# Four transformer layers on one core: biases by TensorE in the joint layers, deviations in eights, the router's places and transfers spread anew, and the first context in eight parts

## Chip, core and metric

One Trainium2 chip, one of its cores. The metric is the time on the device in microseconds (us) of one execution of the whole program. The engines are TensorE (PE in the profile, its weight loads PEld), VectorE (DVE), ScalarE (ACT), GpSimd (POOL) and SyncE (SP), which issues most transfers.

## The reference, cut to what matters

The input x has 64 sequences of 128 tokens with 128 features, the context 64 sequences of 77 tokens. Four layers follow one another, each an attention part and a part of experts:

```
x = x + additive_cross_attention(layernorm(x), context, mask)      # layer 0
x = x + experts16_top4(layernorm(x))                               # layer 0
x = x + cross_attention(layernorm(x), context)                     # layer 1
x = x + experts8_top2(layernorm(x))                                # layer 1
x = x + masked_cross_attention(layernorm(x), context)              # layer 2
x = x + widths_self_attention(layernorm(x))                        # layer 2, its "ffn"
x = x + lowrank_top64_attention(layernorm(x), context)             # layer 3
x = x + experts64_top4_capacity128(layernorm(x))                   # layer 3

# the ends of the two attentions that the change touches
self: outs = xn_o @ o_w[:m, :m].T + o_b[:m]; x = layernorm(x) + outs + x      # 8 heads
low:  out  = (attn @ v) @ Uo @ Vo + bo;       x = x + out                     # 16 heads, top 64 of 77 keys
# the router of the last part
probs = softmax(x @ router_w); top_p, top_i = top_k(probs, 4)
pos = place of each (token, expert) pair among the pairs of its expert; pairs with pos >= 128 go elsewhere
```

A layer norm needs 1/sqrt(var + eps) of every token, that is 64 numbers (one a sequence) in each of 128 partitions.

## The kernel before

The residual stream `X` stays in SBUF, as 64 tiles of 128x128, one a sequence. Each part of a layer is a block of the program in which every engine runs its own written out list of steps, one sequence (or four) a step, and the engines meet through semaphores. A new block begins only when all engines have ended the one before, SyncE with its issues among them.

**Deviations.** VectorE makes mean and variance of all 64 sequences; GpSimd raises them to the power -1/2 (`pow` against a tile of -0.5), since no other engine here does. `norm_gpsimd` (L109) does the first 24 columns (`FIRST`) in the small block that loads the weights, `norm_gpsimd_rest` (L115) the other 40 at the start of the block of steps, ahead of all that GpSimd has to do there. The joint layers need a second power (of the inner norm) and four small operations (`offsets`, L3225 to L3233), on 24 and on 40 columns as well.

**Start.** `load_x` issues the 8 parts of X (L3119), then five constants (L3121). VectorE waits for all constants, makes a bf16 copy of the identity that nothing reads (L3132), and then takes statistics of the 64 sequences (L3136). The block of layer 0's weights (L963) issues nine small loads and then the whole context `l_ctxT`, 2464 KB, in one; the block ends when all have landed, since VectorE waits for them (L980). In layer 0's steps GpSimd adds the text's and the features' halves for half of tanh's input (L1120), which ScalarE waits for (L1068).

**Joint layers** (lines 3155 to 3950). Layer 2's self attention works on sequence a and layer 3's low rank attention on sequence s = a - 9, in the same step, and the router of the last experts runs along in groups of four sequences: c = s // 4 is the group and v = s % 4 the step in it. GpSimd's list in each step is, in this order:

- the router's first part: at v = 0 probabilities and deviations of a group (L2595, L2567 to L2590), at v = 2 `place` (L2614 to L2630), seven operations on 128x256;
- `self_bias(a-2)` (L3762) and `low_bias(s)` (L3766), each 128x128; TensorE waits for both before it adds the results into PSUM with a matmul against the identity (L3415 for the low rank part);
- `self_cut(a+1)` (L3772), for which TensorE waits to project the next self attention;
- `low_distances(s, 0)` (L3778), `self_less_maxima(a)` (L3784), at every fourth step `low_deviations` (L3804 to L3822), `self_spread_k(a+1)` (L3790), `low_distances(s, 1)` (L3778), `low_spread_k(s+1)` (L3797);
- the router's end: at v = 0 `chosen` (L2602, L2609), at v = 2 `fill_rows` (L2636 to L2638), and in each step 4 indirect transfers (L2646), each of which writes 128 rows to the experts' rows in HBM.

The self attention goes round a loop: less maxima(a), then spread k(a+1) on GpSimd, scores(a+1) on TensorE, a copy by ScalarE (L3634), the maxima by VectorE (L3902), less maxima(a+1). VectorE's main work in a step is the selection of the 64 largest of 77 scores for 16 heads in two halves (L3859 to L3886: eight each time), which waits for the distances (L3778).

## Time and profile before

| | |
|---|---|
| time before, median of 3 runs | 3697.84 us (3689.33 to 3698.01) |
| the profiled execution's own time | 3692.36 us |
| its span in the trace | 3690.6 us |
| mean granted clock of TensorE | 0.909 |
| busy: PE, PEld, DVE, ACT, POOL | 2808.8, 1773.2, 2828.7, 2196.2, 2082.5 us |
| start to the first step of layer 0 | 0 to 46.2 us |
| layer 2's cross attention begins | 1867 us |
| joint layers | 2288 to about 3419 us |

The times in all rows are microseconds from the start of the span, unless they say ns. A group of instructions has a line of the kernel, an engine, an operation and its tiles with partitions x elements. A wait in brackets is the time in which the engine was idle before that instruction, and what it was released by. The granted clock is a share of TensorE's full speed.

### The profile page before, as it was taken

How to read it: one execution, taken by the hardware profiler on the slowest of the kernel's cores; microseconds unless marked ns; L12 is line 12 of the kernel's file. 1: busy time of each engine (PE TensorE's matmuls, PEld its weight loads, DVE VectorE, ACT ScalarE, POOL GpSimd, SP SyncE). 2: the span in 40 equal slices, each digit the busy share in tenths (PEclk: the TensorE clock that was granted, in tenths of full speed). 3: DMA queues.
4: the chain of work that ended last, by engine and by line, in shares of the span. 5: the costliest groups of instructions: out<-in, count | busy, mean ns of one | idle time of the engine just before them, and what ended most of it. 6: DMA issues, size and time to landing. Idle time of an engine off the chain costs nothing. (4 is left out here: it accounts for less than half of the span.)

```text
span 3690.6 us, 78369 instructions
## 1 busy us (share of the span) xinstructions
PE 2808.8 (76%) x23589; PEld 1773.2 (48%) x23589; DVE 2828.7 (77%) x11741; ACT 2196.2 (60%) x4429; POOL 2082.5 (56%) x2407
## 2 busy tenths in 40 slices
PE   3777777699979999789669995677777777776267
PEld 1222222344437777544356674455555555554255
DVE  6999999566657788533478885399999999899366
ACT  4999999333326666434246663677677776665130
POOL 5777777200011565747444445545878888777660
PEclk9999999899989999899879997899899998887585
DMA  4332221344420010035410000000111000000037
GB/s 136 119 112 114 100 110 71 83 92 92 92 44 9 27 29 27 31 107 139 123 36 16 15 15 19 3 13 14 40 36 37 21 7 5 5 5 3 1 112 235
DMA packets 179876, 211.46 MB, mean 57 GB/s; under 512 B 73542, under 2 KB 138728, under 8 KB 172039
## 3 DMA queue, kind: packets, MB, share of 16 engines
q1 hardware_dynamic: 146824, 174.31, 16.8%
q0 software_dynamic: 23424, 27.94, 2.3%
q10 hardware_dynamic: 9216, 4.20, 0.4%
q8 instruction: 199, 3.26, 0.4%
q14 instruction: 213, 1.74, 0.2%
HBM read 113.61 MB, written 114.13 MB: 62 GB/s over the span
## 5 line engine op out<-in xcount | busy, mean ns | idle before, releaser
L1068 ACT ACTIVATE l_H<-l_H 128x2048 f32<-128x2048 f32 (+2 forms) x256 | 598.7, 2743 | 2.9 <-POOL l_H L1120 2.7
L1120 POOL TENSOR_TENSOR l_H<-l_feat,l_text 128x4096 f32<-128x4096 f32 x64 | 450.4, 7038 | 131.1 <-PE PS L1024 130.5
L1024 PE MATMUL PS<-l_H,l_wide 128*32 128x512 f32 (+1 forms) x2560 | 330.8, 592 | 164.1 <-ACT l_H L1068 164.1
L1142 DVE TENSOR_TENSOR l_H<-PS,l_text 128x2048 f32<-128x2048 f32 (+1 forms) x192 | 411.7, 2146 | 2.1 <-ACT l_text L1095 2.1
L558 ACT ACTIVATE a_Pr<-PS 77x512 f32<-77x512 f32 x512 | 300.0, 587 | 53.4 <-PE PS L405 53.4
L109 POOL TENSOR_TENSOR RSTD<-norm_tmp,MINUS_HALF 128x24 f32<-128x24 f32 x5 | 20.9, 4190 | 508.6 <-DVE norm_tmp L102 508.6
L2646 POOL DMA_INDIRECT expert_rows<-e3r_row,e3r_rows_at x256 | 254.9, 996 | 89.0 <-issue 74.9
L405 PE MATMUL PS<-IDENT,a_T 128*77 128x128 f32 x2048 | 303.1, 283 | 0.5
L3399 PE MATMUL PS<-IDENT,a_T_l 128*77 128x128 f32 x1024 | 182.2, 308 | 125.3 <-ACT a_Pr_s L3641 101.4
L666 POOL TENSOR_TENSOR a_T<-a_T,a_mx 128x616 f32<-128x616 f32 x128 | 155.6, 1216 | 203.5 <-DVE a_mx L741 203.5
L405 PEld LDWEIGHTS PS<-IDENT,a_T 128*77 128x77 f32 x2048 | 243.0, 153 | 36.7 <-ACT a_yT L544 19.3
L1024 PEld LDWEIGHTS PS<-l_H,l_wide 128*32 128x32 f32 x2560 | 57.4, 109 | 341.1 <-ACT l_H L1068 294.0
L3399 PEld LDWEIGHTS PS<-IDENT,a_T_l 128*77 128x77 f32 x1024 | 129.9, 164 | 179.0 <-ACT a_Pr_s L3641 123.0
L3886 DVE MATCH_REPLACE8 a_T_l<-a_r,a_T_l 128x77 f32<-128x77 f32 x1024 | 213.7, 223 | 0.3 <-issue 0.3
L3867 DVE MATCH_REPLACE8 a_T_l<-a_r,a_T_l 128x77 f32<-128x77 f32 x1024 | 213.7, 223 | 0.3 <-issue 0.3
L2150 POOL DMA_INDIRECT pair_shares<-e_res,e_share_at x156 | 151.6, 972 | 79.7 <-issue 45.1
L3617 ACT ACTIVATE a_Pr_l<-PS 77x512 f32<-77x512 f32 x256 | 151.5, 592 | 74.3 <-PE PS L3399 73.7
L1490 ACT ACTIVATE e_act_g<-PS 128x512 f32<-128x512 f32 x128 | 76.4, 597 | 199.7 <-PE PS L1429 199.5
L3778 POOL TENSOR_TENSOR a_T_l<-a_mx_l,a_T_l 128x616 f32<-128x616 f32 x128 | 155.6, 1216 | 56.4 <-DVE a_mx_l L3896 56.2
L1511 DVE TENSOR_TENSOR e_gu<-e_act_g,PS 128x512 f32<-128x512 f32 x128 | 87.6, 684 | 111.5 <-ACT e_act_g L1490 111.5
L3859 DVE MAX8 a_r<-a_T_l 128x8 f32<-128x77 f32 x1024 | 149.8, 223 | 3.2 <-POOL a_T_l L3778 3.2
L422 PE MATMUL PS<-a_Pr,a_vaug 77*32 77x128 f32 x4096 | 139.4, 276 | 16.9 <-ACT a_OT L597 16.5
(451 smaller groups left out, 8518.6 us busy)
## 6 DMA issues: line engine op xcount, KB each, us to landing
pair_rows<-l_zero SPq DMA_DIRECT2D x35, 1024.0 KB, 5.0
e_wide<-expert_scores SPq DMA_DIRECT2D x32, 1024.0 KB, 9.7
expert_shares<-l_zero SPq DMA_DIRECT2D x16, 1024.0 KB, 5.0
e3c_four<-expert_shares SPq DMA_DIRECT2D x64, 256.0 KB, 3.8
e_xin<-pair_rows SPq DMA_DIRECT2D x39, 264.0 KB, 3.2
e_four<-pair_shares SPq DMA_DIRECT2D x16, 512.0 KB, 4.1
e_w<-in_L_ffn_blocks SPq DMA_DIRECT2D x39, 194.0 KB, 2.5
e3x_xin<-expert_rows SPq DMA_DIRECT2D x32, 200.0 KB
```

The lines of the kernel that those rows point to most:

```text
L405: last = pe.transpose(PS[0:keys, 4 + g % 2, j * S:(j + 1) * S], T[:, u, c:c + keys], m.IDENT[:, :])
L558: act.activation(part, turned, ACT.Exp).then_inc(q[f"P{g}"], 1)
L666: pool.tensor_tensor(t3, t3, bcast(m3, 2, keys), ALU.subtract).then_inc(q[f"T{half}"], 1)
L1024: last = pe.matmul(PS[32 * j:32 * j + 32, 4 + u, 0:cols], wide[:, 32 - r:64 - r], H[:, u, CH * c * S:CH * c * S + cols], start=(r == 0), s ...
L1068: act.activation(cells, cells, ACT.Tanh).then_inc(q[f"tanh{part}"], 1)
L1120: pool.tensor_tensor(H[:, a, lo * S:hi * S].rearrange("p (t f) -> p t f", f=S), bcast(feat[:, a, :], 1, hi - lo), bcast(text[:, a, lo:hi], ...
L1142: dve.tensor_tensor(H[:, u, lo * S:hi * S].rearrange("p (t f) -> p t f", f=S), bcast(PS[:, 1 + u, 0:S], 1, hi - lo), bcast(text[:, u, lo:h ...
L2646: pool.indirect_dma_start(out=m.rows[:, :], out_offset=bass.IndirectOffsetOnAxis(ap=rows_at[:, i % 3, g * K + k:g * K + k + 1], axis=0), i ...
L3399: last = pe.transpose(PS[0:C, 4 + g % 2, j * S:(j + 1) * S], T_l[:, i % 3, c:c + C], m.IDENT[:, :])
L3778: pool.tensor_tensor(t3, bcast(mx_l[:, i % 2, 8 * half:8 * half + 8], 2, C), t3, ALU.subtract) \
L3867: last = dve.match_replace(t3[:, h, :], r1[:, i % 2, 8 * h:8 * h + 8], t3[:, h, :], FAR)
L3886: last = dve.match_replace(t3[:, h, :], r2[:, i % 2, 8 * h:8 * h + 8], t3[:, h, :], FAR)
```

## The change

1. The deviations come in eights: `norm_part(p)` does 8 columns. Part 0 is made in the block of the weights; the others at steps 2, 10, ..., 50 of layers 0, 1 and 2 (at the step's end, ahead of the router's end), all seven in a row at the start of layer 0's experts, and in the joint layers, with the second power and the four small operations, in the GpSimd steps a = 0 to 6, between less maxima(a) and spread k(a+1).
2. The bf16 identity goes, and VectorE's wait for the constants with it. Layer 0's context is issued in eight parts with semaphores of their own, and TensorE waits for a sequence's part.
3. Both biases of the joint layers are added by TensorE, one matmul of the identity and the bias tile each.
4. `place` is split: `slots` stays ahead, `keys` comes after `self_cut`, `far_weights` in the router's end. The 16 transfers of a group go 2, 8, 2, 4 in the steps v = 2, 3, 0, 1, rather than 4 in each.

```diff
-def norm_gpsimd(pool, m): ...
-def norm_gpsimd_rest(pool, m): ...
+def norm_part(pool, m, p):
+    if p == 0:
+        pool.wait_ge(m.s_norm_a, 4 * m.norms + 4)
+    c = slice(EIGHT * p, EIGHT * (p + 1))
+    pool.tensor_tensor(m.RSTD[:, c], m.norm_tmp[:, 0, c], m.MINUS_HALF[:, c], ALU.pow).then_inc(m.s_norm_b, 1)
+def part_due(s):
+    return (s + 6) // EIGHT if s >= 2 and (s + 6) % EIGHT == 0 and s + 6 < B else None
 ...
-            dve.wait_ge(s_const, 16 * len(consts))
-            dve.tensor_copy(m.IDENT_BF[:, :], m.IDENT[:, :])
 ...
-                     (bc[:, 1:2], t[n + "bcb"].partition_broadcast(S)), (ctxT[:, :, :], t["ctxT"])]
+                     (bc[:, 1:2], t[n + "bcb"].partition_broadcast(S))]
+                for p in range(B // EIGHT):
+                    c = slice(EIGHT * p, EIGHT * (p + 1))
+                    sp.dma_start(ctxT[:, c, :], t["ctxT"][:, c, :]).then_inc(q[f"ctx{p}"], 16)
 ...
+                pe.wait_ge(q[f"ctx{i // EIGHT}"], 16)
 ...
+        if have(c - 3 if v >= 2 else c - 4):
+            for k in ((10, 11), range(12, 16), (0, 1), range(2, 10))[v]:
+                scatter(pool, c - 3 if v >= 2 else c - 4, k)
 ...
-                pe.wait_ge(L["bias"], i + 1)
+                pe.matmul(out_ps, m.IDENT[:, :], bo_l[:, :], start=False, stop=False)
                 pe.matmul(out_ps, m.IDENT[:, :], seq(m.X, i), start=False, stop=True).then_inc(L["out"], 1)
 ...
-                pe.wait_ge(Z["y0b"], i + 1)
+                pe.wait_ge(Z["y0"], i + 1)
 ...
+                pe.matmul(out_ps, m.IDENT[:, :], bo_s[:, :], start=False, stop=False)
 ...
             def step(a, s):
                 router.pool_first(pool, s)
-                if real(a - 2):
-                    self_bias(a - 2)
-                if real(s):
-                    low_bias(s)
                 if real(a + 1):
                     self_cut(a + 1)
+                router.pool_middle(pool, s)
                 if real(s):
                     low_distances(s, 0)
                 if real(a):
                     self_less_maxima(a)
                 if a >= 6 and a % 4 == 2 and real(a - 3):
                     low_deviations((a - 6) // 4)
+                if 0 < a + 1 < B // EIGHT:
+                    norm_part(pool, m, a + 1)
+                    offsets(pool, a + 1)
                 if real(a + 1):
                     self_spread_k(a + 1)
```

GpSimd's order at the start of the joint steps, before (L115 and L3225 are the powers on 40 columns, L3772 the cut, L3790 spread k, L3784 less maxima):

```order
L115 TENSOR_TENSOR RSTD<-norm_tmp,MINUS_HALF 128x40
L3225 TENSOR_TENSOR a_in_rstd<-norm_tmp,MINUS_HALF 128x40
L3227 TENSOR_TENSOR a_in_nmr<-MEAN,a_in_rstd 128x40
L3229 TENSOR_SCALAR a_in_nmr<-a_in_nmr 128x40
L3231 TENSOR_TENSOR a_nmr_s<-MEAN,RSTD 128x40
L3233 TENSOR_SCALAR a_nmr_s<-a_nmr_s 128x40
L3772 TENSOR_TENSOR a_xT<-a_xw,WIDTH_FEATURES 128x128
L3790 TENSOR_TENSOR a_kblk_s<-a_kc_s,HEAD 128x256
L3772 TENSOR_TENSOR a_xT<-a_xw,WIDTH_FEATURES 128x128
L3784 TENSOR_TENSOR a_T_s<-a_T_s,a_mx_s 128x1024
```

And with the change (L112 and L3238 are the powers, L3775 the cut, L3793 spread k, L3787 less maxima):

```order
L3775 TENSOR_TENSOR a_xT<-a_xw,WIDTH_FEATURES 128x128
L3793 TENSOR_TENSOR a_kblk_s<-a_kc_s,HEAD 128x256
L3775 TENSOR_TENSOR a_xT<-a_xw,WIDTH_FEATURES 128x128
L3787 TENSOR_TENSOR a_T_s<-a_T_s,a_mx_s 128x1024
L112 TENSOR_TENSOR RSTD<-norm_tmp,MINUS_HALF 128x8
L3238 TENSOR_TENSOR a_in_rstd<-norm_tmp,MINUS_HALF 128x8
L3240 TENSOR_TENSOR a_in_nmr<-MEAN,a_in_rstd 128x8
L3242 TENSOR_SCALAR a_in_nmr<-a_in_nmr 128x8
L3244 TENSOR_TENSOR a_nmr_s<-MEAN,RSTD 128x8
L3246 TENSOR_SCALAR a_nmr_s<-a_nmr_s 128x8
L3793 TENSOR_TENSOR a_kblk_s<-a_kc_s,HEAD 128x256
L3775 TENSOR_TENSOR a_xT<-a_xw,WIDTH_FEATURES 128x128
```

The two powers on 40 columns and their four small operations, which stood ahead of the first cut, now stand as seven portions of 8 columns, each behind less maxima and ahead of spread k.

GpSimd's order from the end of a step v = 2 over the step v = 3 into v = 0, in the stretch in which the router runs along, before (L3778 are the distances):

```order
L2638 TENSOR_SCALAR e3r_rows_at<-e3r_skeytop 128x16
L2646 DMA expert_rows<-e3r_row,e3r_rows_at 8192x200 x4
L3762 TENSOR_TENSOR a_y<-a_y,a_bo_s 128x128
L3766 TENSOR_TENSOR X<-X,a_bo_l 128x128
L3772 TENSOR_TENSOR a_xT<-a_xw,WIDTH_FEATURES 128x128
L3778 TENSOR_TENSOR a_T_l<-a_mx_l,a_T_l 128x616
L3784 TENSOR_TENSOR a_T_s<-a_T_s,a_mx_s 128x1024
L3790 TENSOR_TENSOR a_kblk_s<-a_kc_s,HEAD 128x256
L3778 TENSOR_TENSOR a_T_l<-a_mx_l,a_T_l 128x616
L3797 TENSOR_TENSOR a_kblk_l<-a_kc_l,HEAD 128x308
L2646 DMA expert_rows<-e3r_row,e3r_rows_at 8192x200 x4
L2595 TENSOR_TENSOR e3r_row<-e3r_row,e3r_rec 128x4x64
```

And with the change (L3781 are the distances, L2653 the transfers, L2598 and L2570 the start of step v = 0):

```order
L2646 TENSOR_SCALAR e3r_rows_at<-e3r_skeytop 128x16
L2653 DMA expert_rows<-e3r_row,e3r_rows_at 8192x200 x2
L3775 TENSOR_TENSOR a_xT<-a_xw,WIDTH_FEATURES 128x128
L3781 TENSOR_TENSOR a_T_l<-a_mx_l,a_T_l 128x616
L3787 TENSOR_TENSOR a_T_s<-a_T_s,a_mx_s 128x1024
L3793 TENSOR_TENSOR a_kblk_s<-a_kc_s,HEAD 128x256
L3781 TENSOR_TENSOR a_T_l<-a_mx_l,a_T_l 128x616
L3800 TENSOR_TENSOR a_kblk_l<-a_kc_l,HEAD 128x308
L2653 DMA expert_rows<-e3r_row,e3r_rows_at 8192x200 x8
L2598 TENSOR_TENSOR e3r_row<-e3r_row,e3r_rec 128x4x64
```

Both bias additions are gone from the step's head, and v = 3 ends with eight transfers where it had four.

## Rows read from the trace of the kernel before

**Rows 1.** Timeline of the start: start us, us, engine line op, tiles, count, [idle <- releaser].
```profile
...
0.75 11.20 SPq L3119 DMA_DIRECT2D X<-in_x  x8
...
14.68 0.91 SPq L3121 DMA_DIRECT2D HEAD<-in_c_head  x2
18.52 0.23 DVE L3132 CAST IDENT_BF<-IDENT 128x128 bf16<-128x128 f32 x1 [18.52 <-DMA HEAD<-in_c_head]
18.67 12.46 DVE L3136 BATCH_NORM_STATS2 STATS<-X 128x6 f32<-128x128 f32 x64
31.40 0.33 SPq L963 DMA_DIRECT2D l_Ws<-in_L_xattn_Ws  x1
...
35.09 0.43 SPq L963 DMA_DIRECT2D l_ctxT<-in_ctxT  x1
...
45.57 0.15 DVE L980 COPY l_wide<-l_w 128x1 f32<-128x1 f32 x1 [12.51 <-DMA l_ctxT<-in_ctxT]
...
46.22 6.76 POOL L115 TENSOR_TENSOR RSTD<-norm_tmp,MINUS_HALF 128x40 f32<-128x40 f32 x1 [7.10 <-POOLq L953]
...
60.40 3.62 ACT L1068 ACTIVATE l_H<-l_H 128x4096 f32<-128x4096 f32 x1 [2.65 <-POOL l_H L1120]
```

**Rows 2.** DMA issues of 0 to 60 us: KB each, median us from issue to landing.
```profile
...
X<-in_x SPq DMA_DIRECT2D x8, 512.0 KB, 7.2
```

**Rows 3.** Timeline where layer 2's cross attention begins.
```profile
...
1862.02 4.20 POOL L109 TENSOR_TENSOR RSTD<-norm_tmp,MINUS_HALF 128x24 f32<-128x24 f32 x1 [52.75 <-DVE norm_tmp L102]
...
1864.78 0.15 DVE L287 TENSOR_SCALAR a_bqs<-a_bq 128x1 f32<-128x1 f32 x1
...
1867.24 6.78 POOL L115 TENSOR_TENSOR RSTD<-norm_tmp,MINUS_HALF 128x40 f32<-128x40 f32 x1 [0.34 <-POOLq L228]
```

**Rows 4.** Timeline of GpSimd (and one row of ScalarE) where the joint layers begin.
```profile
...
2288.55 6.79 POOL L115 TENSOR_TENSOR RSTD<-norm_tmp,MINUS_HALF 128x40 f32<-128x40 f32 x1 [5.99 <-POOLq L3235]
...
2289.70 0.46 ACT L3624 ACTIVATE a_xw<-PS,a_nb,a_nw 128x128 f32<-128x128 f32 x1 [0.57 <-PE PS L3428]
...
2303.40 0.45 POOL L3772 TENSOR_TENSOR a_xT<-a_xw,WIDTH_FEATURES 128x128 f32<-128x128 f32 x1
...
2310.94 1.90 POOL L3784 TENSOR_TENSOR a_T_s<-a_T_s,a_mx_s 128x1024 f32<-128x1024 f32 x1 [2.56 <-DVE a_mx_s L3902]
...
2317.20 1.90 POOL L3784 TENSOR_TENSOR a_T_s<-a_T_s,a_mx_s 128x1024 f32<-128x1024 f32 x1 [3.38 <-DVE a_mx_s L3902]
...
2359.62 1.90 POOL L3784 TENSOR_TENSOR a_T_s<-a_T_s,a_mx_s 128x1024 f32<-128x1024 f32 x1 [2.45 <-DVE a_mx_s L3902]
```

**Rows 5.** Windows of the joint stretch: length, busy of PE, PEld, DVE, ACT, POOL, clock.
```profile
...
2666.00:3206.97 540.97, 411.21 (x4202) 302.69 (x4205) 507.25 (x3550) 387.55 (x993) 454.12 (x682) 0.90 0.07 19
2863.10:2881.50 18.40, 12.90 (x144) 9.59 (x140) 17.35 (x117) 13.60 (x33) 16.44 (x22) 1.00 0.05 14
2881.50:2893.30 11.80, 9.89 (x119) 7.29 (x120) 11.51 (x82) 9.97 (x31) 10.72 (x14) 1.00 0.06 18
2893.30:2911.90 18.60, 13.19 (x138) 9.48 (x139) 18.24 (x138) 14.98 (x37) 16.08 (x29) 1.00 0.04 10
2911.90:2928.50 16.60, 12.77 (x130) 9.71 (x128) 16.24 (x112) 9.63 (x26) 13.52 (x23) 0.79 0.20 56
```

**Rows 6.** VectorE's two longest waits in 2666 to 3206.97: total, times, longest.
```profile
...
DVE a_mx_s L3902 <- ACT a_T_s L3634: 10.2, 7, 2.0
...
DVE e3r_mn L2686 <- ACT e3r_nl L2522: 7.9, 4, 2.4
```

**Rows 7.** GpSimd's groups by line in 2666 to 3206.97.
```profile
...
L2646 POOL DMA_INDIRECT expert_rows<-e3r_row,e3r_rows_at x128 | 127.8, 999 | 43.0 <-issue 36.7 <-POOL e3r_rows_at L2638 6.3
...
L3762 POOL TENSOR_TENSOR a_y<-a_y,a_bo_s 128x128 f32<-128x128 f32 x32 | 14.9, 465 | 0.2
L3766 POOL TENSOR_TENSOR X<-X,a_bo_l 128x128 f32<-128x128 f32 x32 | 14.8, 462 | 0.0
```

**Rows 8.** TensorE's matmuls against the identity at L3415: ns min/median/max.
```profile
...
L3415 PE MATMUL PS<-X,IDENT x128: 275/377/583, 2326.2 to 3310.7; 128*128 128x128 f32 x128
```

142 lines of the change are left out of this document (63 added, 79 removed), and 2 rows, old and new, of the table L.

## The prediction, made before the change was run

> **What bounds the kernel now.** I first read the timeline of the start [rows 1]. For 18.52 us VectorE does nothing: it waits for the last constant. Its 64 statistics then take 12.46 us, the weights' block starts at 31.40, and VectorE waits there again, 12.51 us, for the context. Only at 46.22 do the steps start, and GpSimd first spends 6.76 us on the power of 40 columns. Nothing runs beside these waits, so what is saved here shortens the whole. Then I looked where the joint layers begin [rows 4]: GpSimd's first cut comes at 2303.40, 14.85 us after its first power at 2288.55, and no other engine has work. The rows after it show a loop: less maxima starts at 2310.94, at 2317.20 and, for the eighth sequence, at 2359.62, and each time GpSimd was idle for 2.5 to 3.4 us before it, until VectorE had the maxima. Last I read the windows of the joint stretch in which the router runs along [rows 5]: 540.97 us for 32 steps, VectorE busy 507.25, GpSimd 454.12, TensorE 411.21. VectorE sets the pace there; it is idle 33.7 us in all, and its two longest waits are 10.2 and 7.9 us [rows 6].
>
> **The start.** Without the wait for constants VectorE starts on X as its parts land. X is issued from 0.75 us over 11.20 us and a part lands 7.2 us after its issue [rows 1, 2], so the last is there by about 18. The parts' statistics take 12.46 / 8 = 1.6 us each, and seven can be done before that. They end near 19.2 instead of 31.13: **-11.9**. The constants are issued by 15.6 and are not late for anything after it. The weights' block then starts at 19.5. Its nine small loads go from 31.40 to 35.09, 0.46 apart, and now eight issues follow in place of one, 7 x 0.47 = 3.3 us more for SyncE. In the old times the last weight lands near 38 and SyncE is done at 38.9, so the steps could start at 39.2 instead of 46.2: **-7.0**. The context's first part, issued at 35.1, is hardly ever late for it; if it takes X's 7.2 us it lands at 42.3, and the gain is 4 instead of 7. The Trainium skill (SBUF — State Buffer, "The DMA setup-cost knee") speaks against the split, since each transfer has a fixed cost of some 2 us and one should use the largest; by its fit, an estimate, the first part of 308 KB would land in 2.7 us and eight in a row take 22 us. The trace's one transfer of 2464 KB took 10.5 us, and only its first eighth is waited for here.
>
> GpSimd is free 6.8 us sooner in layer 0's first step, where ScalarE waited 2.65 us for it [rows 1]: **-2.6**, at most -3.7, at least 0.
>
> **Deviations elsewhere.** The price of a power comes from these rows: 24 columns 4.20, 40 columns 6.76 to 6.79 us [rows 1, 3, 4]; that is 0.16 us a column and 0.3 fixed, so 8 columns take about 1.65. Where layer 2 begins, GpSimd's power of 24 columns ran from 1862.02 to 1866.2, VectorE was done at 1864.9 and the steps started at 1867.2 [rows 3]: **-2.0**. The other blocks wait for weights there: 0. The parts within the steps of layers 0, 1 and 2 take 2.2 us each and lie beside tanh or the softmax; where GpSimd is near the pace, in layer 2, some 0.2 of each shows: **+1**.
>
> **The joint layers' first steps.** Removed: the wait of 14.85 us ahead of the first cut. ScalarE's tile for it was written by 2290.2 [rows 4], so 13.2 us go, and less maxima of the first sequence would start at 2297.7. Added: a portion of two powers (3.3 us) and four small operations, 4.5 us (before, the four made up what 14.85 leaves beside two powers of 6.79, 1.3 on 40 columns), in each of seven steps. It stands behind less maxima(a) and ahead of spread k(a+1), which is right inside the loop. A step of the loop took (2359.62 - 2310.94) / 7 = 6.95 us [rows 4], and since GpSimd's idle time in it lies after spread k and is spent waiting for what spread k starts, none of the 4.5 us is hidden by it; only the bias that goes, 0.4 us, may give something back. I take 10.95 us a step, 0.5 given back: the eighth less maxima at 2297.7 + 7 x 10.95 = 2374.4 instead of 2359.62, **+15**. Bounds: +18 if nothing at all is given back, +8 if another 1 us a step is given back, and -13 if the portions were fully hidden.
>
> **The router's stretch.** On GpSimd two additions go from each step. By busy time they are 29.7 us in 32 steps [rows 7]; their start-to-start distance is 0.41 us each, which makes 26.5. (The Trainium skill, Perfetto Trace Analysis, "GPSIMD Engine Instruction", says to time GpSimd by start-to-start spacing and not by spans; the sum would be 3 us larger by the spans, on an engine that does not set the pace.) A transfer takes (127.8 + 36.7) / 128 = 1.29 us [rows 7]. The four steps took 18.4, 11.8, 18.6 and 16.6 us for v = 2, 3, 0, 1 [rows 5]. Moving two transfers (2.6 us) out of v = 2, four (5.1) into v = 3 and two out of v = 0, and taking 0.8 for biases from each, GpSimd could do them in about 15.1, 16.0, 15.3 and 15.8 against VectorE's busy 17.35, 11.51, 18.24 and 16.24. So the four together can only fall to VectorE's 63.3 from 65.4. The additions thus come off the path only as far as they shorten VectorE's waits. Those were 18.1 us in the two rows named [rows 6] and 33.7 in all. I take most of the named ones and nothing of the rest: **-16**. Bounds: -33.7, and 0 to the other side if ScalarE or TensorE, not GpSimd, is what VectorE waits for. TensorE gets two matmuls a step, 0.38 us each at the median and 0.58 at most [rows 8], 0.76 x 32 = 24 us of work beside 411.21 busy of 540.97: hidden by its idle time, and without this cover half of it would show, +12, which is in the second rival.
>
> At the end of the joint layers eight transfers of the last group stand ahead of the last group's probabilities instead of four: 4 x 1.29 = 5.2 us, part of it covered: **+2**.
>
> **The sum.** -11.9 - 7.0 - 2.6 - 2.0 + 1 + 15 - 16 + 2 = **-21.5**. From the profiled execution's 3692.36 that gives 3670.9; that execution is 5.5 us under the median of the runs shown, 3697.84, from which it would be 3676.3. I say **3673**.
>
> **The rivals.**
>
> *A. VectorE loses all its waits* in the router's stretch, -33.7 instead of -16: total -39, 3654 to 3659. For it: GpSimd's order is now even, and VectorE had 17.35 of 18.4 us busy already. Against it: part of the idle time is waits for ScalarE. 0.15.
>
> *B. The steady stretch gains nothing.* VectorE waits for ScalarE's copies [rows 6], and these come after TensorE, which now has more to do. Total -5.5, 3687 to 3692, or with half of the matmuls showing +6.5. 0.15.
>
> *C. The joint start's portions are hidden* behind VectorE's other work: -13 instead of +15, total -49, 3643 to 3648. Against it: nothing else of VectorE's runs before a = 9. 0.08.
>
> *D. Slower: the eight transfers.* Between the second distances of v = 3 and the first cut of v = 0 stand eight transfers, 10.3 us instead of 5.2 [rows 7]. VectorE's backlog covers that while it has a selection's half to do, and the step of v = 3 is the one in which it has least, 11.51 us [rows 5]. The two steps v = 3 and v = 0 took 30.4 us and GpSimd now needs 31.3 in them, 1.5 more than VectorE's 29.75. If the late cut also makes the self attention's maxima late by a round of TensorE and ScalarE, 3.5 us a group, it is 13 groups x 3.5 = +46 in place of -16: total -5.5 + 46 = +40, 3732. It decides from 0.4 us a group on, where the sum passes zero. 0.08.
>
> *E. The start does not shorten* since X, not the constants, lands last, or the weights' block waits for the context's parts: the 18.9 us of the first two terms go, total -2.6, 3690 to 3695. Against it: the constants are issued behind X. By the rule of the largest transfer (Trainium skill, as above) this would be the case if all eight parts were waited for. 0.06.
>
> **How the numbers follow.** The forecast has 0.48, A 0.15, B 0.15, C 0.08, D 0.08, E 0.06. The range takes in the forecast with its bounds, A and most of B: 3650 to 3692. Within 0.3%, 11 us, is what a measurement of this kernel can't tell from no change. Faster by more: forecast, A, C and a small part of B, 0.76. Same: most of B and of E, 0.15. Slower: D and B's far end, 0.09.
>
> **What would show it.** In the profile after, the first statistics should start before 10 us, the steps of layer 0 near 27, GpSimd's first cut in the joint layers within 2 us of the block's start, and less maxima 10 to 11 us apart for seven steps. VectorE should be busy over 95% in the router's stretch, and v = 3 should be longer and v = 2 and 0 shorter. The forecast is wrong if less maxima keeps its 7 us (C), if VectorE's waits for GpSimd grow at v = 0 (D), or if the router's stretch keeps its 16.9 us a step (B).

## The result, and the profile after

The changed kernel took 3685.89 us, median of 12 runs (3676.86 to 3691.37), the kernel before beside it 3697.74 (12 runs): ratio 0.9973, 95% interval 0.9961 to 0.9984. That is 12 us less, where 25 less were forecast. Measured once more at the end, it gave 0.9976 (0.9967 to 0.9985). The profiled executions have spans of 3690.6 and 3683.9 us, 6.7 apart; I split these 6.7, and take verdicts from the medians.

The timeline of the start, after (L972 to L980 are VectorE's preparations in the weights' block, L1094 is ScalarE's copy of the first features):

```profile
...
4.82 1.65 DVE L3148 BATCH_NORM_STATS2 STATS<-X 128x6 f32<-128x128 f32 x8 [4.82 <-DMA X<-in_x]
...
17.48 1.64 DVE L3148 BATCH_NORM_STATS2 STATS<-X 128x6 f32<-128x128 f32 x8 [0.17 <-DMA X<-in_x]
19.73 0.33 SPq L959 DMA_DIRECT2D l_Ws<-in_L_xattn_Ws  x1
...
23.42 4.30 SPq L962 DMA_DIRECT2D l_ctxT<-in_ctxT  x8
27.52 0.15 DVE L979 COPY l_wide<-l_w 128x1 f32<-128x1 f32 x1 [6.12 <-DMA l_bc<-in_L_xattn_bcb]
...
28.17 0.20 POOL L1109 TENSOR_TENSOR l_mr<-MEAN,RSTD 128x8 f32<-128x8 f32 x1 [3.25 <-POOLq L949]
...
31.03 0.28 ACT L1094 ACTIVATE l_feat<-PS 128x128 f32<-128x128 f32 x1 [1.23 <-PE PS L1009]
```
Against [rows 1]: the statistics start at 4.82 instead of 18.67 and end at 19.12. The weights' block starts at 19.73. SyncE is done with the eight context issues at 27.72, VectorE, which waits until 27.52 for the last small weight, with its two copies at 27.87, and the steps start at 28.17 instead of 46.22; that is 18.05 us (18.9 forecast). The next part, layer 0's experts, starts at 659.9 instead of 680.1: -20.2, where -21.5 was forecast.

GpSimd's timeline where the joint layers begin:

```profile
...
2269.16 0.45 POOL L3775 TENSOR_TENSOR a_xT<-a_xw,WIDTH_FEATURES 128x128 f32<-128x128 f32 x1 [12.86 <-ACT a_xw L3638]
...
2276.71 1.90 POOL L3787 TENSOR_TENSOR a_T_s<-a_T_s,a_mx_s 128x1024 f32<-128x1024 f32 x1 [2.56 <-DVE a_mx_s L3905]
2278.56 1.67 POOL L112 TENSOR_TENSOR RSTD<-norm_tmp,MINUS_HALF 128x8 f32<-128x8 f32 x1
2280.20 1.64 POOL L3238 TENSOR_TENSOR a_in_rstd<-norm_tmp,MINUS_HALF 128x8 f32<-128x8 f32 x1
...
2287.30 1.90 POOL L3787 TENSOR_TENSOR a_T_s<-a_T_s,a_mx_s 128x1024 f32<-128x1024 f32 x1 [3.38 <-DVE a_mx_s L3905]
...
2353.82 1.90 POOL L3787 TENSOR_TENSOR a_T_s<-a_T_s,a_mx_s 128x1024 f32<-128x1024 f32 x1 [3.38 <-DVE a_mx_s L3905]
```
Against [rows 4]: the block starts at 2267.5, 21.1 us sooner than before. The first cut no longer waits for the powers, only for ScalarE. The first less maxima comes at 2276.71, 34.2 sooner. Then two powers stand behind each less maxima, and six steps in a row are 10.59 us long. The seventh takes 13.58 us, since `low_deviations`, ten operations of some 3 us in all, stand in it as well; before, it was the longest of the seven too, with 8.75. The eighth less maxima is at 2353.82, only 5.8 us sooner than before. So 13.1 us were won ahead of the loop and 28.4 lost in it, +15.3 together, where +15 was forecast.

The windows and the waits of the router's stretch, from the 28th to the 60th less maxima as before [rows 5, 6]:

```profile
...
2662.53:3203.41 540.88, 410.39 (x4323) 309.20 (x4322) 506.41 (x3554) 386.39 (x992) 428.08 (x618) 0.90 0.07 19
```
```profile
...
PE PS L3495 <- POOL a_xT L3775: 31.2, 8, 4.3
...
POOL a_T_l L3781 <- DVE a_mx_l L3899: 20.0, 15, 1.9
...
DVE a_mx_s L3905 <- ACT a_T_s L3648: 15.2, 8, 2.9
...
DVE e3r_skeytop L2739 <- POOL e3r_skey L2632: 8.6, 8, 1.4
...
PE PS L3371 <- POOL a_kblk_l L3800: 4.1, 7, 0.6
```
Here is the miss: 540.88 us for the 32 steps, against 540.97 before, where 16 less were forecast. GpSimd is busy 26 us less, and nothing came of it. VectorE's work is the same, 506.4. Its waits have only moved: the one for the router's minima (7.9) is gone, but the one for the self attention's maxima is 15.2 instead of 10.2, and the one for the place's keys is 8.6. TensorE's waits have moved as well. It waits 31.2 us for the cut in eight times, that is one a group of four steps, at v = 0, and only 4.1 us for the low rank part's spread k (L3800). In the same stretch of the kernel before these were:

```profile
...
PE PS L3358 <- POOL a_kblk_l L3797: 30.4, 15, 3.5
...
PE PS L3481 <- POOL a_xT L3772: 12.3, 9, 1.8
```
Where the late cut comes from is seen in GpSimd's timeline over one step v = 3 and the start of v = 0:

```profile
...
2808.86 1.22 POOL L3781 TENSOR_TENSOR a_T_l<-a_mx_l,a_T_l 128x616 f32<-128x616 f32 x1 [1.86 <-DVE a_mx_l L3899]
...
2814.57 1.22 POOL L3781 TENSOR_TENSOR a_T_l<-a_mx_l,a_T_l 128x616 f32<-128x616 f32 x1 [1.19 <-DVE a_mx_l L3899]
...
2816.60 1.01 POOL L2653 DMA_INDIRECT expert_rows<-e3r_row,e3r_rows_at  x1 [0.15 <-issue]
...
2830.20 0.46 POOL L3775 TENSOR_TENSOR a_xT<-a_xw,WIDTH_FEATURES 128x128 f32<-128x128 f32 x1
```
In v = 3 GpSimd is idle for 3.9 us in three waits for VectorE (the third, of 0.84 us, is that of less maxima), so it isn't loaded to its limit there. But from the second distances at 2814.57 on, everything up to the next cut follows without a pause: spread k, the eight transfers, the probabilities and the deviations, 15.6 us in all.

What follows such a wait is seen in windows of 3 us around it, in one group (columns: busy of PE, PEld, DVE, ACT, POOL, then the granted clock):

```profile
...
2824.85:2827.85 3.00, 1.09 (x6) 0.67 (x6) 2.93 (x14) 1.15 (x3) 2.60 (x7) 1.00 0.09 28
2827.85:2830.85 3.00, 0.06 (x1) 0.09 (x1) 3.00 (x21) 0.00 (x0) 2.70 (x9) 0.88 0.00 0
2830.85:2833.85 3.00, 3.00 (x24) 2.36 (x25) 2.85 (x28) 0.79 (x3) 3.00 (x3) 0.50 0.00 0
2833.85:2836.85 3.00, 3.00 (x39) 2.29 (x38) 3.00 (x25) 1.89 (x7) 3.00 (x4) 0.50 0.06 13
2836.85:2839.85 3.00, 3.00 (x15) 1.85 (x15) 2.85 (x28) 2.99 (x9) 2.26 (x6) 0.50 0.01 3
2839.85:2842.85 3.00, 3.00 (x35) 2.42 (x31) 2.56 (x14) 2.12 (x4) 1.12 (x2) 0.91 0.18 62
2842.85:2845.85 3.00, 1.37 (x16) 0.86 (x8) 1.57 (x5) 2.91 (x6) 1.90 (x3) 1.00 0.00 0
```
```profile
...
2830.80 0.77 PE L3495 MATMUL PS<-a_xT,a_Wk_s 128*128 128x128 f32 x2 [4.34 <-POOL a_xT L3775]
```
TensorE is nearly idle for 4.34 us until the cut. In the 3 us in which it was idle the clock falls, and in the 9 us after it is 0.50, 1.2 GHz instead of 2.4. In them it does what VectorE waits for next: the wait for the self maxima ends at 2844.28, after 1.80 us, and at 2842.85 to 2845.85 VectorE is busy for 1.57 of 3 us.

### The profile page after: what moved, and what is told of

The parts are those of the page before. It is cut to its first block and busy times, and to the rows that moved or that the text cites. A ratio compares the mean times of both kernels' runs of the same rounds, so it can differ in the third digit from the quotient of the medians.

```text
span 3683.9 us, 79075 instructions
## 1 busy us (share of the span) xinstructions
PE 2829.7 (77%) x23845; PEld 1802.6 (49%) x23845; DVE 2824.5 (77%) x11740; ACT 2194.5 (60%) x4429; POOL 2052.6 (56%) x2370
## 5 line engine op out<-in xcount | busy, mean ns | idle before, releaser
L112 POOL TENSOR_TENSOR RSTD<-norm_tmp,MINUS_HALF 128x8 f32<-128x8 f32 x40 | 66.3, 1662 | 496.6 <-DVE norm_tmp L102 491.9
L2653 POOL DMA_INDIRECT expert_rows<-e3r_row,e3r_rows_at x256 | 254.8, 995 | 90.1 <-issue 74.7
L3781 POOL TENSOR_TENSOR a_T_l<-a_mx_l,a_T_l 128x616 f32<-128x616 f32 x128 | 155.5, 1216 | 79.7 <-DVE a_mx_l L3899 79.7
L3787 POOL TENSOR_TENSOR a_T_s<-a_T_s,a_mx_s 128x1024 f32<-128x1024 f32 x64 | 121.4, 1896 | 58.1 <-DVE a_mx_s L3905 58.1
## 6 DMA issues: line engine op xcount, KB each, us to landing
e_wide<-expert_scores SPq DMA_DIRECT2D x32, 1024.0 KB, 10.2
```

The source lines that it names most:

```text
L2653: pool.indirect_dma_start(out=m.rows[:, :], out_offset=bass.IndirectOffsetOnAxis(ap=rows_at[:, i % 3, k:k + 1], axis=0), in_=rows_of(i)[:, ...
L3781: pool.tensor_tensor(t3, bcast(mx_l[:, i % 2, 8 * half:8 * half + 8], 2, C), t3, ALU.subtract) \
```

## The experiments

From here on "32 steps" is the time from the 28th to the 60th less maxima of the self attention in each profile. "Over" and "under" are differences of medians, and ratios are to the kernel before on the same chip.

### Even transfers

```diff
-            for k in ((10, 11), range(12, 16), (0, 1), range(2, 10))[v]:
+            for k in (range(8, 12), range(12, 16), range(0, 4), range(4, 8))[v]:
```

> The changed kernel with four transfers in each step again instead of 2, 8, 2, 4. Theory L (late cut: the eight transfers and the deviations stand ahead of v = 0's cut, so VectorE waits for the self attention's maxima at v = 1): these eight waits of 1.9 us (15.2 in the stretch of 32 steps) go, the 32 steps fall from 540.9 to about 528 us, total about 16 us under the changed kernel. Theory T (TensorE's two added matmuls a step lengthen the chain that VectorE waits for): 32 steps stay within 2 us of 540.9. Theory P (the order of before had its waits at the place's keys, and the even transfers bring them back): 32 steps at 540 to 545, with waits for the router's minima of 7 to 8 us again.

```profile
...
2654.95:3180.66 525.71, 408.96 (x4332) 308.61 (x4320) 506.25 (x3554) 388.15 (x994) 430.09 (x617) 0.92 0.07 20
```
```profile
...
DVE e3r_skeytop L2739 <- POOL e3r_skey L2632: 4.8, 7, 1.1
DVE a_mx_s L3905 <- ACT a_T_s L3648: 3.9, 7, 1.4
```
3669.66 us, ratio 0.9928 (0.9912 to 0.9945), 16 us under the changed kernel. The 32 steps took 525.7, and the waits for the self maxima fell from 15.2 to 3.9. Theory L was right in both numbers, theories T and P were not: the uneven transfers take back the 15 us that the rest of the change had won in these steps. From the second distances of v = 3 to the cut of v = 0 it is now 10.6 us (2803.32 to 2813.88) instead of 15.6, and TensorE waits there no longer.

### Biases on GpSimd again

```diff
-                pe.matmul(out_ps, m.IDENT[:, :], bo_l[:, :], start=False, stop=False)
+                pe.wait_ge(L["bias"], i + 1)
...
+                if real(a - 2):
+                    self_bias(a - 2)
+                if real(s):
+                    low_bias(s)
```

> The changed kernel with both biases on GpSimd again, as before. GpSimd has 0.83 us more in each step. Theory L: the cut at v = 0 comes another 0.8 us later, the wait at v = 1 grows from 1.9 to 2.7, 32 steps take 547 us or more, total +8 to +15 us over the changed kernel. Theory T: TensorE is relieved and the 32 steps take 530 to 538 us, total 5 to 12 us under it.

```profile
...
2660.67:3212.32 551.65, 402.17 (x4179) 297.91 (x4171) 507.94 (x3554) 385.89 (x991) 455.55 (x681) 0.89 0.07 19
```
3705.62 us, ratio 1.0023 (1.001 to 1.0036), 20 us over the changed kernel, more than expected. The 32 steps took 551.7, 10.8 more. So the moved biases do help, even beside the uneven transfers.

### Portions of deviations outside the loop

```diff
-                if 0 < a + 1 < B // EIGHT:
-                    norm_part(pool, m, a + 1)
-                    offsets(pool, a + 1)
                 if real(a + 1):
                     self_spread_k(a + 1)
...
                     low_spread_k(s + 1)
+                if a == 2 or 9 <= a < 15:
+                    p = 1 if a == 2 else a - 7
+                    norm_part(pool, m, p)
+                    offsets(pool, p)
```

> The changed kernel with the seven portions of deviations in the joint layers at the end of GpSimd's steps a = 2 and a = 9 to 14 instead of inside the loop of a = 0 to 6. If the 4.5 us of each portion lie on the loop, as the prediction has it, less maxima goes back to about 6.9 us a step, the eighth starts 26 to 29 us sooner (relative to the first), and the total falls by 25 to 28 us. Rival: the steps from a = 9 on are paced by something that does not start sooner, and 10 us or less come through.

```profile
...
2282.76 1.90 POOL L3787 TENSOR_TENSOR a_T_s<-a_T_s,a_mx_s 128x1024 f32<-128x1024 f32 x1 [2.56 <-DVE a_mx_s L3906]
...
2295.48 1.90 POOL L3787 TENSOR_TENSOR a_T_s<-a_T_s,a_mx_s 128x1024 f32<-128x1024 f32 x1 [2.04 <-DVE a_mx_s L3906]
...
2297.91 1.67 POOL L112 TENSOR_TENSOR RSTD<-norm_tmp,MINUS_HALF 128x8 f32<-128x8 f32 x1
2299.54 1.64 POOL L3238 TENSOR_TENSOR a_in_rstd<-norm_tmp,MINUS_HALF 128x8 f32<-128x8 f32 x1
...
2333.36 1.90 POOL L3787 TENSOR_TENSOR a_T_s<-a_T_s,a_mx_s 128x1024 f32<-128x1024 f32 x1 [2.97 <-DVE a_mx_s L3906]
```
3663.01 us, ratio 0.9908 (0.9891 to 0.9924), 23 us under the changed kernel. The first and the eighth less maxima are 50.6 us apart instead of 77.1: the 26.5 us expected. The one portion left in these steps stands behind spread k, where GpSimd idled, and costs 1.9 us (50.6 against the 48.7 of the kernel before). Nearly all of the gain reached the end.

### Router's probabilities and deviations behind the cut

```diff
     def pool_first(pool, s):
-        if v == 0 and have(c - 3) and c - 3 < late_weighed:
-            probabilities(pool, c - 3)
-        if v == 0 and have(c - 2):
-            deviations(pool, c - 2)
-            pads(pool, c - 2)
...
     def pool_middle(pool, s):
+        if v == 0 and have(c - 3) and c - 3 < late_weighed:
+            probabilities(pool, c - 3)
+        if v == 0 and have(c - 2):
+            deviations(pool, c - 2)
+            pads(pool, c - 2)
```

> The changed kernel with the router's probabilities and deviations at v = 0 behind the cut instead of ahead of it. Theory L: the cut at v = 0 comes 3.7 us sooner, TensorE's wait for it (31.2 us in 8 times) goes nearly, VectorE's waits of 15.2 us for the self maxima go, the 32 steps take about 528 us, total about 14 us under the changed kernel. Theory T: 32 steps stay within 2 us of 540.9. The router's own chain is 0.5 us later, which should not show.

```profile
...
2657.63:3191.89 534.26, 417.31 (x4333) 314.38 (x4326) 506.57 (x3554) 387.76 (x995) 428.90 (x617) 0.90 0.07 19
```
3679.99 us, ratio 0.9956 (0.994 to 0.9973), 6 us under the changed kernel; 14 were expected. The 32 steps took 534.3. TensorE's wait for the cut went from 31.2 to 2.0 us, and that for the maxima from 15.2 to 7.6. So the cut behind the deviations is less than half of the cost of the uneven transfers (6.6 of 15.2 us). The move also puts the distances of v = 0 no sooner than they were; I read the rest as GpSimd's work in the two steps being more than VectorE's, which no run shows by itself and the run with six transfers below speaks against. So the rest is not explained.

### The place in one piece

```diff
-            slots(pool, c - 3)
+            slots(pool, c - 3)
+            keys(pool, c - 3)
+            far_weights(pool, c - 3)
```

> Four transfers a step, and the router's place in one piece again ahead of the cut at v = 2; the biases stay on TensorE. Against the same with the place split (525.7 us for the 32 steps, total 3669.7): the cut at v = 2 comes 2.8 us later. If the same holds for v = 2 as for v = 0 (a late cut is paid at the next step's maxima), 32 steps take 530 to 536 us and the total is 3675 to 3682. Rival: only the cut at v = 0 matters, since VectorE has its backlog at v = 2, and the 32 steps stay at 525 to 527.

```profile
...
2665.61:3188.47 522.86, 402.19 (x4326) 300.84 (x4322) 506.37 (x3553) 387.42 (x993) 429.22 (x617) 0.94 0.07 20
```
3670.36 us, ratio 0.992 (0.9895 to 0.9945): the same as with the split place (3669.66). The 32 steps took 522.9 in this profile, 2.8 less than with it. The split brings nothing that can be seen; what I expected of a late cut at v = 2 did not come. As this kernel differs from the one before, in the router's stretch, in the biases alone, these account for 541.0 - 522.9 = 18.1 us there, by one profile of each. That one profile can be off by as much is seen below, where the same 32 steps once take 540.7; that the biases help at all rests also on the medians, of the run above with them on GpSimd (20 us) and of this one, 30 us under the kernel before.

### Both at once, and more of the same

Even transfers and late portions together:

> Four transfers a step and the joint layers' seven portions of deviations at the end of the steps a = 2 and 9 to 14. If the two gains (16 us from even transfers, 23 from the portions' place) are separate, since one lies in the first 8 steps and the other in the router's stretch, the total is 3644 to 3649 us: ratio 0.986. Rival: they share a cause, and 3655 or more remain.

3643.31 us, ratio 0.9855 (0.9836 to 0.9874), within a microsecond of the 3644 to 3649 expected. The two gains are separate and add.

The same with the probabilities and deviations behind the cut:

> As the kernel with even transfers and late portions, with the router's probabilities and deviations behind the cut at v = 0 as well. With even transfers VectorE's waits in the 32 steps were 9 us (3.9 for the self maxima, 4.8 for the place's keys). Theory L says that at most the 3.9 can still go: 32 steps 522 to 526, total 0 to 5 us under the kernel without this move. Rival: the late distances of v = 0 now cost more, and the total rises by 1 to 4 us.

3642.73 us, ratio 0.9846 (0.9823 to 0.9869), no difference; the 32 steps took 526.0 in both profiles. With four transfers ahead of it, the cut at v = 0 was not late for anyone: TensorE has no wait over 0.6 us for it in either profile.

### What the two matmuls cost

Both bias matmuls are taken out, so the output lacks both biases:

```diff
-                pe.matmul(out_ps, m.IDENT[:, :], bo_l[:, :], start=False, stop=False)
-                pe.matmul(out_ps, m.IDENT[:, :], bo_s[:, :], start=False, stop=False)
```

> Four transfers a step and neither bias of the joint layers added by any engine (the output lacks both): what the two matmuls a step cost. Theory L: TensorE has room, 32 steps stay within 1.5 us of 525.7 and the total within 3 us of 3669.7. Theory T: half of the 24 us of added matmuls shows, 32 steps at 514 to 520.

```profile
...
2656.49:3181.80 525.31, 396.04 (x4194) 293.10 (x4192) 506.12 (x3554) 390.09 (x993) 429.75 (x618) 0.92 0.07 20
```
3664.49 us, ratio 0.9911 (0.9889 to 0.9934), 5 us under the kernel with them where at most 3 were expected, but less than the spread of either. The 32 steps took 525.3 against 525.7 us, with TensorE busy 13 us less (the prediction had 24 us of work for the 64 matmuls). TensorE hides them: theory T falls.

### Even transfers, the place in one piece, late portions

> Four transfers a step, the place in one piece ahead of the cut, and the joint layers' portions at the end of steps a = 2 and 9 to 14. The stretch of 32 steps was 522.9 with the place in one piece and 525.7 with it split, so this should be 3 to 5 us under the kernel with the split place (3643.3): 3637 to 3641, ratio 0.984. Rival: the 2.8 us are a chance pattern of one alignment, and 525 or more come back: 3643.

```profile
...
2625.79:3166.52 540.73, 425.89 (x4327) 321.04 (x4325) 507.26 (x3553) 386.39 (x993) 428.43 (x617) 0.89 0.07 19
```
3637.81 us, ratio 0.9832 (0.9815 to 0.9848): the fastest version, 61 us under the kernel before. But its times went from 3634.31 to 3650.36, and its profile is of a long one: 540.7 us for 32 steps that are, instruction by instruction, those of the kernel that took 522.9. Groups of four steps took 68.2 to 68.6 us up to about 3036 us, and 65 to 66 after it. In a slow group the windows of TensorE, with the wait ahead of them and the one after, look like this (the same columns; then a row of TensorE and one of VectorE):

```profile
...
2762.27:2765.27 3.00, 2.98 (x38) 2.25 (x34) 3.00 (x30) 1.35 (x6) 3.00 (x4) 0.51 0.02 5
2765.27:2768.27 3.00, 3.00 (x33) 2.57 (x25) 2.50 (x19) 1.28 (x4) 2.21 (x6) 0.50 0.06 13
2768.27:2771.27 3.00, 3.00 (x17) 1.84 (x16) 2.43 (x22) 1.98 (x6) 2.39 (x3) 0.50 0.12 39
2771.27:2774.27 3.00, 3.00 (x31) 2.52 (x27) 2.88 (x18) 1.85 (x3) 1.22 (x2) 0.78 0.19 66
2774.27:2777.27 3.00, 1.74 (x17) 1.13 (x16) 1.20 (x2) 2.88 (x6) 1.63 (x2) 1.00 0.00 0
```
```profile
...
2761.28 0.46 PE L3496 MATMUL PS<-a_xT,a_Wk_s 128*128 128x128 f32 x2 [2.20 <-POOL a_xT L3776]
```
```profile
...
2776.07 1.22 DVE L3907 TENSOR_REDUCE a_mx_s<-a_T_s 128x8 f32<-128x1024 f32 x1 [1.85 <-ACT a_T_s L3649]
```
TensorE had waited 2.20 us for the cut at v = 2, its clock is 0.50 for over 9 us, and VectorE then waits 1.85 us for the self maxima that came late. In this profile's last group, of 65.1 us, windows of 3 us show 0.50 only from 3155 to 3158, and 0.77 and 0.66 from 3143 to 3149, and VectorE has no wait over 0.6 us. So the slow groups have the pattern of the changed kernel at v = 0, in a kernel without its cause. They seem to belong to the execution and not to the kernel: the profiled one took 3650.36 us at a mean clock of 0.908, the three others of the same kernel 3634.31 to 3638.52 at 0.913 to 0.915.

### Six transfers

```diff
+            for k in (range(8, 12), range(12, 16), range(0, 2), range(2, 8))[v]:
```

> As the last, with 2, 6, 4, 4 transfers in the steps v = 2, 3, 0, 1. Where does a long run of transfers ahead of v = 0's cut begin to cost? If at the point where GpSimd's v = 3 and v = 0 together exceed VectorE's 30 us: with six transfers they need 31.3 as with eight less 2.6 us plus 2.6 for the two more at v = 0, so the pair is as long as with eight, and 32 steps take 533 to 541. If only the run ahead of the cut counts, half of the loss comes: 528 to 532. If six are free: 522 to 525.

3647.23 us, ratio 0.9856 (0.9839 to 0.9873), 9 us over the same with four a step. The 32 steps took 531.4, which lies among the 528 to 532 of "half of the loss". But the eight groups took 68.7, 65.4, 65.2, 70.9, 65.2, 65.5, 65.4 and 65.2 us, so the number fits, but not for that reason. Six groups are as fast as with four transfers a step, though TensorE waits 1.4 to 1.6 us for the cut of v = 0 in nearly all; the two slow ones have the pattern of the last section, a late cut at v = 2 and late self maxima behind it (waits of 1.7 and 2.4 us). That six transfers cost anything at v = 0 is therefore not shown. What this run does show is that the sum over the two steps isn't the price: GpSimd has the same ten transfers in v = 3 and v = 0 as in the changed kernel, where all eight groups took 66.6 us or more, and 533 to 541 us were expected if the sum counted. With six, it is 13.1 us from the second distances to the cut (2783.45 to 2796.55), with eight 15.6, and TensorE's wait is 3.5 to 4.3 us.

### The uneven transfers in the kernel before

```diff
-        if v < 2 and have(c - 4):
-            scatter(pool, c - 4, v + 2)
-        if v >= 2 and have(c - 3):
-            scatter(pool, c - 3, v - 2)
+        if have(c - 3 if v >= 2 else c - 4):
+            scatter(pool, c - 3 if v >= 2 else c - 4, ((10, 11), range(12, 16), (0, 1), range(2, 10))[v])
```

> The kernel before with transfers 2, 8, 2, 4 and nothing else changed, the biases still on GpSimd. With the place split and biases on GpSimd the 32 steps took 551.7. Theory L: the uneven transfers cost 10 to 18 us here too: 32 steps 551 to 560, total 13 to 22 us over the kernel before. Rival: they belong with the longer GpSimd step of v = 2 and help while GpSimd is the tighter engine: 530 to 540.

3712.07 us, ratio 1.0041 (1.0025 to 1.0058), 13 us over the kernel before; 32 steps in 557.4. The uneven transfers cost about the same there, 16 us by this profile, as in the changed kernel; but the profile is that of the longest of the five executions (3720.82).

### The context in one transfer, awaited by TensorE

> As the kernel with even transfers, the place in one piece and late portions, with layer 0's context in one transfer of 2464 KB again, but awaited by TensorE in the steps and not by VectorE ahead of them. SyncE is free 3.3 us sooner, so the steps begin near 27.6 instead of 28.1; the context took 10.5 us, so it lands near 33.9, where TensorE's first use is at 30.4: the first features come 3 to 4 us later, and the total is 2 to 4 us higher. Rival: the transfer is spread so that it lands by 30.5: no difference, and the whole gain is that nobody waits for all of it.

```profile
...
33.83 0.77 PE L1006 MATMUL PS<-l_yT,l_W 128*128 128x128 f32 x2 [4.46 <-DMA l_ctxT<-in_ctxT]
...
34.98 0.28 ACT L1092 ACTIVATE l_feat<-PS 128x128 f32<-128x128 f32 x1 [4.87 <-PE PS L1007]
```
```profile
...
2640.27:3163.01 522.74, 404.47 (x4319) 303.18 (x4313) 506.27 (x3553) 386.62 (x992) 429.19 (x618) 0.93 0.07 20
```
3644.4 us, ratio 0.9852 (0.9834 to 0.9869), 7 us over the same kernel with eight parts. TensorE waits 4.46 us for the whole context, and the first features come at 34.98 instead of the 31.18 of the kernel above: 3.8 us are what the split gives there. By the statistics' sums at the start of layer 0's experts (L93) it is 5.6 us, 658.3 against 652.7. The rest of the seven that I had put on this edit is that VectorE no longer waits for the context ahead of the steps. (Against the 7 us between the medians stand spreads of 7 us and more.)

One expectation failed here: SyncE was free some 4 us sooner, its last issue being over at 23.67, and yet the steps began at 28.47 and not near 27.6.

```profile
...
27.82 0.15 DVE L977 COPY l_wide<-l_w 128x1 f32<-128x1 f32 x1 [6.61 <-DMA l_bc<-in_L_xattn_bcb]
```
VectorE waits until 27.82 for the last small weight, issued at 22.76 to 23.19. So it is this weight that the steps wait for, not SyncE.

The 32 steps of this kernel took 522.7, at a clock of 0.93, and are the same as those of the kernel above with 540.7 at 0.89.

### Matmuls against the clock's fall, which settled nothing

12 matmuls that nobody reads, ahead of the changed kernel's wait for the cut at v = 0:

```diff
+                if i - 1 - DELTA >= 12 and (i - 1 - DELTA) % 4 == 0:
+                    for _ in range(12):
+                        pe.matmul(k_ps, m.IDENT[:, :], bo_s[:, :], start=True, stop=True)
                 pe.wait_ge(Z["xT"], i + 1)
```

> The changed kernel (2, 8, 2, 4 transfers) with 12 idle matmuls of the identity on TensorE ahead of its wait for the cut in each step v = 0 of the router's stretch; they write PSUM columns that the projection overwrites. In the changed kernel TensorE idles 4.3 us there, and its granted clock is then 0.50 for about 11 us, while it makes the scores. Theory C (the late cut costs by way of the clock): the 12 matmuls fill 3 to 4 us of the idle time, the clock stays at 1.00 after it, VectorE's waits for the self maxima fall from 15 to under 6 us, and the 32 steps fall from 540.9 to 525 to 532, total 8 to 16 us under the changed kernel. Theory L (the lateness of the cut alone, one round of TensorE and ScalarE, makes the wait): 32 steps stay at 538 to 543.

> The changed kernel with 12 idle matmuls ahead of TensorE's wait for the cut at v = 0, once more, since the last execution fell on a chip where VectorE and ScalarE paused for other reasons and the kernel before took 3896 us. On a chip where the kernel before takes about 3697 us: theory C says full clock after the cut and 32 steps of 525 to 532 us, total 3670 to 3678; theory L says 538 to 543 and 3683 to 3689. If the matmuls only push the half clock to a later place, VectorE's wait moves with it and 32 steps take 535 or more.

```profile
...
DVE a_mx_s L3908 <- ACT a_T_s L3651: 30.7, 24, 2.8
DVE a_T_l L3873 <- issue: 20.4, 38, 1.2
```
The two runs took 3902 and 3900 us, on two chips where the kernel before takes 3896 and 3893: ratios 1.0023 (1.0005 to 1.0042) and 1.0021 (1.0002 to 1.004). VectorE has pauses there between the instructions of its selection that no other engine releases ("issue", 20.4 us in 38 times in this stretch; 0.3 us in the profiles of the other chips), and groups take 75 us instead of 67. TensorE has another pause there, up to 7.4 us, in which it waits for ScalarE's `a_xw`, the tile that is to be cut; in one group the clock is at 0.50 from 2868.9 to 2877.9, ahead of the added matmuls, which run from 2878.14 to 2882.09. So these don't compare with the rest. Only the changed kernel on such a chip could tell whether the matmuls help; its run for this came to a chip with 3696 us for the kernel before:

> The changed kernel itself, unedited, to have it on the chip on which the kernel with the 12 idle matmuls ran (kernel before 3893 us, with matmuls ratio 1.0022 and 1.0021). Theory C: it is slower than the kernel with the matmuls, ratio 1.004 or more there. Theory L: it is equal or faster, ratio 0.997 to 1.002. On a chip where the kernel before takes 3697 us it gives 0.997 again and tells nothing new.

3686.72 us, ratio 0.9976 (0.9967 to 0.9985), 537.7 us for 32 steps, every group of them between 66.6 and 67.6. In the first profile they were 66.6 to 68.5. So groups slower than the 65.1 to 66.1 of the kernels with even transfers are the changed kernel's rule, not an accident of one profile. Whether the fall of the clock or the lateness of the cut alone makes them stays open.

The fastest version with such matmuls at v = 2, and that version itself, twice more:

> The kernel with even transfers, the place in one piece and late portions, with idle matmuls at v = 2: 8 ahead of the wait for the low rank keys and 6 ahead of the wait for the cut. Its stretch of 32 steps was once 540.7 and in the same steps of two other kernels 522.7 and 522.9, where the slow groups of four (68.3 us instead of 65.2) have the clock at half in the 12 us ahead of and over the self scores. Theory C: with TensorE kept at work all groups take 65 to 65.6, and the total is 3631 to 3637, with less spread. Rival: the clock falls after busy stretches too, and more work makes it fall more: 68 us groups, 3645 or more.

> The kernel with even transfers, the place in one piece and late portions once more. If the slow groups come and go between executions of one kernel, its times spread over 3633 to 3650 again, and this profile's groups are another mixture of 65.2 and 68.3 us; the median should be 3636 to 3641.

> The kernel with even transfers, the place in one piece and late portions once more, for the same reason. On a chip where the kernel before takes about 3697 us: median 3636 to 3641, ratio 0.983 to 0.985. If slow groups come and go between executions, this profile's groups of four are another mixture of 65.2 and 68.3 us than the last (seven of 68.3 and three of 65).

All three ran on those two slower chips: 3872.21 us with the matmuls, ratio 0.9938 (0.9916 to 0.9959), and 3864.43 without on the same chip, 0.9923 (0.9903 to 0.9942); on the second chip 3860.89 without, 0.9926 (0.9902 to 0.995). The matmuls bring nothing there. The version itself is 0.75% under the kernel before on these chips, and 1.7% on the first. Whether its slow groups come and go from one execution to the next was not seen directly, with one profile a run; for it speak the times and clocks of its four executions above, and that the same steps took 522.7, 522.9 and 540.7 us in three profiles.

## Why the prediction was wrong, by its own steps

- **The start**: -11.9, -7.0 and -2.6 forecast, -20.2 measured against -21.5. The times are right. The reason for the second term is not: I had SyncE as the last (38.9 in the old times, 27.7 now) and the last weight near 38, but the weight landed as late as SyncE was done, and with SyncE free some 4 us sooner the steps began no sooner (28.47). That the two came out within 0.2 us of each other is luck. (The small loads are eight; I had written nine.)
- **Deviations elsewhere**: -2.0 and +1 forecast. Where layer 2 begins, the time from the statistics' first sum (L93) to the first step fell from 6.64 us (1860.58 to 1867.22) to 4.84 (1842.03 to 1846.87), that is -1.8: right. The lead went from 20.2 us at 659.9 to 21.1 at the joint layers, but this says little: in the twelve profiles whose kernels have the same program up to there and that ran on the faster chips, the first cut comes anywhere between 2263.2 and 2276.0 (with the context in one transfer at 2275.4, within that). So the +1 can't be read from them.
- **The joint layers' first steps**: +15 forecast, +15.3 measured, and the portions' place was shown as its cause by moving them. Right in mechanism and in size, with six steps at 10.59 us and the seventh, which has the low rank deviations too, at 13.58, where I had 10.95 for each.
- **The router's stretch**: -16 forecast, -0.1 measured. This is the step that failed: "So the four together can only fall to VectorE's 63.3 from 65.4". It took for granted that the new order on GpSimd costs nobody anything as long as its sum over the four steps stays under VectorE's. For v = 3 and v = 0 I had written down that GpSimd needs 31.3 us where VectorE has 29.75, and yet gave that mechanism to rival D alone, with 0.08. (The 15.1 to 15.8 us a step are the steps' lengths with the moved work taken off, not GpSimd's work, of which the rows show less.) It wasn't the sum that cost either: GpSimd works 30.8 us in these two steps of the changed kernel and is idle 3.9 more in v = 3. What the eight transfers did was to put the cut of v = 0 15.6 us behind the second distances, so that TensorE waited for it. By the run with the deviations behind the cut this late cut is worth 6.6 of the 15.2 us; even transfers bring all 15.2 back, and how the rest comes about is open.

  The runs split the term: the biases bring -18.1, close to the -16 that I gave to the stretch as a whole, the split of the place is between 0 and +3, and the transfers 2, 8, 2, 4 cost +15. Of these the +15 is the firmest, since the executions with and without the uneven transfers don't overlap (3664.83 to 3671.13 and 3676.86 to 3691.37 us); the other two carry the doubt of single profiles named above.

  And even the -18.1 isn't the fall from 65.4 to 63.3 that I forecast: the group that I had read with 65.4 us was among the fastest of the kernel before, whose eight groups took 70.0, 68.8, 66.2, 65.5, 65.4, 68.9, 66.2 and 70.0 us. In no profile did one of the eight groups take less than 65.1. What the moved biases gave is that the slow groups went.

  Rival D had the right place, the wait for the self maxima after v = 0, and the right trigger; its price per group was 3.5 us and is 15.2 / 8 = 1.9. Its sum over the two steps isn't borne out, since six transfers keep the sum and six groups of eight lose nothing. Rival D held in a kernel whose biases had moved, so both happened together, and neither the forecast nor rival B (nothing gained, since TensorE or ScalarE is the limit) describes it, although B gives the time.
- **TensorE's added matmuls**: forecast as hidden, and they are (0.4 us in 32 steps); their work was put too high, 24 us for the 13 by which TensorE's busy time changes.
- **The end**: +2 forecast for the last group's transfers; from the last less maxima to the end it took 414.3 instead of 415.1 us. Nothing was lost there.
- From the 8th to the 28th less maxima, where the router's steps begin, 2.3 us were lost that the sum did not have, and 2.3 won between the 60th and the last.

The sum from the profiles: -21.1 - 13.1 + 28.4 + 2.3 - 0.1 - 2.3 - 0.8 = -6.7. With -16 for the stretch it would have been -22.6, near the forecast's -21.5. The -21.1 is uncertain by some 6 us either way, as said under the second point; so is the agreement. The medians, 12 us apart, are the better measure of the whole.

The Trainium skill's two rules, weighed ahead: on the largest transfer (SBUF — State Buffer, "The DMA setup-cost knee") the measurement decides for the split here, 31.18 against 34.98 us to the first features, since what counts is when the first eighth lands; the rule is about the rate. Timing GpSimd by start-to-start spacing (Perfetto Trace Analysis, "GPSIMD Engine Instruction") agrees with the busy time's fall: 26.0 us less in 32 steps, 26.5 by spacing and 29.7 by spans; what the loss of busy time brought was 18 us.

## What to carry to other kernels

When work is moved between the steps of a periodic schedule, don't compare the engines by their sums over the period, nor over two steps: follow what now stands between the last thing that such an engine waits for and the next thing that others wait for from it. Here GpSimd was under VectorE over the period and even idle in v = 3, and yet the cut came 5 us later behind its second distances (15.6 instead of 10.6), and 15 us in 32 steps were lost with the eight transfers, some 7 of them by this cut; with the same sum in another order most groups lost nothing. A piece of work that must be done early but not now belongs into the steps where its engine idles while another sets the pace, not inside the loop that all wait for: the same seven portions cost 28 us inside the loop, and moving them gave 23 back. Before reading a gain from one group of steps, look at all of them: the 65.4 us that the forecast started from were among the fastest of eight. Build the parts of a combined change apart; here one of four took back the gain of another.
